# Three PSUM pairs instead of two for the first attention pass, and squares of the q/k norm moved from VectorE to ScalarE

## The chip, the cores and the metric

One Trainium2 chip, all 8 cores. Each core runs the same program on half of one batch element's queries. The metric is the device time in microseconds (us) of the slowest core. Engines: PE (TensorE), DVE (VectorE), ACT (ScalarE), POOL (GpSimd), SP (SyncE, used here for DMA).

## The reference

Two transformer layers in sequence, each attention, add, layernorm, feed-forward, add, layernorm. The change touches only the attention of layer 0:

```
q = quat_norm(quat_linear(x, qW, qb))     # r,i,j,k quarters of 256 features
k = quat_norm(quat_linear(x, kW, kb))     # each divided by sqrt(r*r + i*i + j*j + k*k + eps)
v = quat_linear(x, vW, vb)
scores = einsum(q, k) * Dh**-0.5 + const  # 16 heads of 64, 4096 keys
attn = softmax(scores);  out = einsum(attn, v)
```

The input is 4 x 4096 x 1024. A core computes 2304 query positions (2048 and a margin for the windowed attention of layer 1) against all 4096 keys.

## The kernel before, in words

The program is a list of operations for each engine, in the order in which they are appended. An engine runs its list strictly in that order; operations of different engines are joined by semaphore waits given by hand. Every VectorE and ScalarE operation also waits for the one before it on its own engine to have finished.

**The q/k stage** (`proj_norm`, called 13 times: 8 tiles of 512 positions for k, 4 of 512 and one of 256 for q). For a tile, PE makes eight output chunks `oc` of 128 features, 8 matmuls each (line 331), into PSUM banks 0 to 3 in turn. DVE takes each out with the bias into `P1FS1(oc)` (line 335), and only this frees the bank, so PE can be at most four chunks ahead. Then, for each half `h` of the 256 features of a quarter, the norm needs the sum of squares of chunks h, h+2, h+4, h+6: DVE squares chunk h into `P1FS2(h)` (line 345), then three times squares the next chunk into one temporary in PSUM bank 6 (`P1FS2(2)`, line 350) and adds it (line 353). ACT makes exp(-0.5 ln(sum + eps)) of it (lines 354 and 357). Last, DVE multiplies all eight chunks by the result of their half (line 364), in the order of `oc`, so the halves alternate. The take-outs of the next tile are behind this on DVE's list.

**Attention** (`emit_p1c(g, ...)`, called for head group g = 0 and g = 1, 8 heads each). There are 6 tiles `qt` of 384 queries, and for each 16 batches `j` (4 head pairs by 4 quarters of the keys). `emit_A(j)` is the score part: for 8 key blocks `sq`, two matmuls of 64 rows (line 506, one per head of the pair, called a score pair below) into one set of two PSUM banks, then one ACT exponential over both (line 518, 128x768) into SBUF. `emit_P(j)` is the value part: 48 matmuls of 65 columns (line 548) into bank 6 or 7. PE's order in a tile is A(0), A(1), then P(j), A(j+2) for each j, and P(14), P(15) with nothing between. The score sets alternate over two sets (banks 0, 1 and banks 2, 3): a score pair waits for the exponential that last read its set:

```python
par = (j * 8 + sq) % 2
set_base = 2 * par
if state["exp_prev"][par]:
    fw.append(state["exp_prev"][par])
```

In the pass g = 0 nothing uses banks 4 and 5. In the pass g = 1 a hook (`p2_pump`) puts the output projection, quantization and feed-forward of layer 0 between the batches, and those use banks 4 and 5. After each `qt` the result goes by DMA to DRAM (`ATT0`). Between the passes, the v projection for the second group (`emit_p1b(1, ...)`) waits for the first pass to be over. The later stages (layer 1) follow.

Of the kernel before, what the change touches and what calls it, by code (L numbers as in the profile page):

```python
# [9 lines left out]
AF = mybir.ActivationFunctionType  # L10
ALU = mybir.AluOpType
# [83 lines left out]
def build_program(stage="full"):  # L95
# [29 lines left out]
    sch = Sched()  # L125
# [3 lines left out]
    with (  # L129
# [35 lines left out]
        def P1FS1(c, n):  # L165
            return TY2.bitcast(F32)[:, 53248 // 4 + c * 512: 53248 // 4 + c * 512 + n]
# [27 lines left out]
        def PB(b, a, n, dt=None):  # L194
            if dt is not None:
# [15 lines left out]
                       waits=[tJ])  # L211
# [5 lines left out]
                      waits=[t_csum])  # L217
# [4 lines left out]
                      waits=[t_crep])  # L222
# [25 lines left out]
        def quat_bias_row(dst_off, B_ap, as_f32r_off=None, final_extra=()):  # L248
# [16 lines left out]
            if as_f32r_off is not None:  # L265
# [10 lines left out]
                       waits=[dm_chain[-1]])  # L276
# [32 lines left out]
        def proj_norm(si, n, src_fn, wbig_off, bias_col, dst_fn, extra_first=()):  # L309
            p = si % 2  # L310
            dsem = "dx0" if p == 0 else "dx1"
            tld = None
            for ic in range(8):
                wt = [stg_free[p]] if stg_free[p] else []
                tld = sch.dma("g", dsem, (lambda g, s_=src_fn(ic), d_=XSG(p, ic, 0, n):
                                          g.dma_start(out=d_, in_=s_)), waits=wt)
            ev = []
            for oc in range(8):
                bank = oc % 4
                last_mm = None  # L320
                for ic in range(8):
                    wt = []
                    if ic == 0:
                        wt = [tld] + list(extra_first)
                        if psum_free.get(bank):
                            wt.append(psum_free[bank])
                    lhsT = TEV(wbig_off, BF16, 8 * D)[:, ic * D + oc * 128: ic * D + oc * 128 + 128]
                    rhs = XSG(p, ic, 0, n)
                    last_mm = sch.op("t", (lambda t, o_=PB(bank, 0, n), l_=lhsT, r_=rhs,
                                           s0=(ic == 0), s1=(ic == 7):  # L330
                                           t.matmul(o_, l_, r_, start=s0, stop=s1)),  # L331
                                     mark=(ic == 7), waits=wt)
                ev.append(sch.op("v", (lambda v, d_=P1FS1(oc, n), p_=PB(bank, 0, n),
                                       b_=BIASB[:, bias_col + oc: bias_col + oc + 1]:
                                       v.tensor_scalar(d_, p_, b_, None, ALU.add)),
                                 waits=[last_mm]))
                psum_free[bank] = ev[-1]
            stg_free[p] = sch.op("t", lambda t: t.nop(), mark=True)

            out_toks = []  # L340
            for h in range(2):
                ssum = P1FS2(h, n)
                wt = [ev[h]] + ([norm_free[0]] if norm_free[0] else [])
                t0 = sch.op("v", (lambda v, d_=ssum, a_=P1FS1(h, n):
                                  v.scalar_tensor_tensor(d_, a_, 1.0, a_, ALU.mult, ALU.mult)),
                            waits=wt)
                for j in (2, 4, 6):
                    tmp = P1FS2(2, n)
                    sch.op("v", (lambda v, d_=tmp, a_=P1FS1(h + j, n):
                                 v.scalar_tensor_tensor(d_, a_, 1.0, a_, ALU.mult, ALU.mult)),  # L350
                           waits=[ev[h + j]])
                    t0 = sch.op("v", (lambda v, d_=ssum, a_=tmp:
                                      v.tensor_tensor(d_, d_, a_, ALU.add)))
                t2 = sch.op("s", (lambda s, d_=ssum: s.activation(d_, d_, AF.Ln,
                                                                  bias=BIASB[:, 62:63])),
                            waits=[t0, t_eps6])
                t3 = sch.op("s", (lambda s, d_=ssum: s.activation(d_, d_, AF.Exp, scale=-0.5)),
                            waits=[t2])
                out_toks.append(t3)
            final = None  # L360
            for oc in range(8):
                h = oc % 2
                final = sch.op("v", (lambda v, d_=dst_fn(oc), a_=P1FS1(oc, n), b_=P1FS2(h, n):
                                     v.tensor_tensor(d_, a_, b_, ALU.mult)),
                               waits=[out_toks[h]])
            norm_free[0] = final
            return final
# [10 lines left out]
        for sj in range(5):  # L378
            n = 512 if sj < 4 else 256
            q_done = proj_norm(  # L380
                8 + sj, n,
                (lambda ic, s_=sj, n_=n: XSF[128 * ic:128 * ic + 128, 512 * s_:512 * s_ + n_]),
                0, 0,
                (lambda oc, s_=sj, n_=n: QBUF(oc, 512 * s_, n_)))
# [12 lines left out]
        tkq_nop = sch.op("t", lambda t: t.nop(), mark=True)  # L397
# [3 lines left out]
        def quat_w2(dst_off, W_ap, firstw):  # L401
            lastv = [firstw] * 4
            tok = None
            for ic in range(8):
                comp, half = ic // 2, ic % 2
                for ob in range(4):
# [18 lines left out]
                         waits=[q_done, tkq_nop])  # L425
# [49 lines left out]
                xsg2_free = sch.op("t", lambda t: t.nop(), mark=True)  # L475
            return done, xsg2_free

        def emit_p1c(g, ready, state, hook=None):
            PVB = (6, 7)
            for qt in range(NQT):  # L480
                batches = [(hp, H, half) for hp in range(4)
# [3 lines left out]
                def emit_A(j, qt=qt, batches=batches, etoks=etoks):  # L485
                    hp, H, half = batches[j]
                    kch = g * 4 + hp
                    toks = []
                    for sq in range(8):
                        par = (j * 8 + sq) % 2  # L490
                        set_base = 2 * par
                        fw = []
                        if state["exp_prev"][par]:
                            fw.append(state["exp_prev"][par])
                        if qt == 0 and j == 0 and sq == 0:
                            fw += list(ready)
                        sub = H * 16 + half * 8 + sq
                        last = None
                        for hh in (0, 1):
                            bank = set_base + hh  # L500
                            lhsT = KBUF(kch, sub * 128, 128, p0=64 * hh, np_=64)
                            rhs = QBUF(kch, qt * QT, QT, p0=64 * hh, np_=64)
                            w = fw if hh == 0 else []
                            last = sch.op("t", (lambda t, o_=PB(bank, 0, QT), l_=lhsT,
                                                r_=rhs, tp=(64 * hh, 0):
                                                t.matmul(o_, l_, r_, start=True, stop=True,  # L506
                                                         tile_position=tp)),
                                          waits=w, mark=(hh == 1))
                        ew = [last]
                        if state["expt_free"][j % 2]:  # L510
                            ew.append(state["expt_free"][j % 2])
                        tile0 = (j % 2) * 16 + sq * 2
                        in_ap = PALL[:, set_base * 512: set_base * 512 + 1024].rearrange(
                            "p (b x) -> p b x", x=512)[:, :, 0:QT]
                        out_ap = TE[:, tile0 * QT: (tile0 + 2) * QT].rearrange(
                            "p (b x) -> p b x", x=QT)
                        etok = sch.op("s", (lambda ss, o_=out_ap, i_=in_ap:
                                            ss.activation(o_, i_, AF.Exp,  # L518
                                                          bias=BIASB[:, 63:64], scale=0.125)),
                                      waits=ew)  # L520
                        state["exp_prev"][par] = etok
                        toks.append(etok)
                    etoks[j] = toks
# [59 lines left out]
                for qs in range(3):  # L583
                    sp = sch.dma("y", "dsp", (lambda y, r0=qt * QT + qs * 128,
                                              a_=ATMv(qs * 512, 512), g_=g:
                                              y.dma_start(out=ATT0[r0:r0 + 128, g_ * 512:(g_ + 1) * 512],
                                                          in_=a_)),
                                 waits=[state["pv_norm"]])
                state["atm_free"] = sp
                if hook:  # L590
                    hook(3 * qt + 2, 4)
            return state

        st_p1c = {"exp_prev": {0: None, 1: None}, "pv_norm": None,
                  "expt_free": [None, None], "atm_free": None,
                  "pvfree": {6: None, 7: None}}
        v_done0, xf0 = emit_p1b(0, [t_vones])
        st_p1c = emit_p1c(0, [v_done0, tkq_nop, q_done], st_p1c)
        tg0 = sch.op("t", lambda t: t.nop(), mark=True)
        g0_exps = [t for t in (st_p1c["exp_prev"][0], st_p1c["exp_prev"][1]) if t]  # L600
        v_done1, xf1 = emit_p1b(1, [st_p1c["atm_free"], st_p1c["pv_norm"]])
        st_p1c["atm_free"] = xf1

# [294 lines left out]
        st_p1c = emit_p1c(1, [v_done1], st_p1c, hook=p2_pump)  # L898
# [52 lines left out]
        for ic in range(8):  # L951
# [7 lines left out]
                        waits=[l_b1q])  # L959
# [643 lines left out]
```

How the kernel before makes its waits and increments, by code:

```python
        def run(engobj, eng):  # L66
            for waits, fn, incsem, incval in self.ops[eng]:
                for (sn, sv) in waits:
                    engobj.wait_ge(sems[sn], sv)
                inst = fn(engobj)
                if incsem is not None:
                    inst.then_inc(sems[incsem], incval)
# [22 lines left out]
def build_program(stage="full"):  # L95
# [285 lines left out]
                8 + sj, n,  # L381
                (lambda ic, s_=sj, n_=n: XSF[128 * ic:128 * ic + 128, 512 * s_:512 * s_ + n_]),
                0, 0,
                (lambda oc, s_=sj, n_=n: QBUF(oc, 512 * s_, n_)))
        if stage == "p1a":
            for c in range(8):
                sch.dma("g", "dout", (lambda g, c_=c, q_=QBUF(c, 0, SPAN): g.dma_start(
                    out=DBG[:, c_ * SPAN: (c_ + 1) * SPAN],
                    in_=q_)), waits=[q_done, k_done])
            sch.op("y", lambda y: y.wait_ge(sem_handles["dout"], sch.cnt["dout"]))
            sch.emit(block, sem_handles)
            stack.close()
            return nc
# [511 lines left out]
            for sl in range(NSL):  # L906
                sch.dma("g", "dout", (lambda gg, sl_=sl: gg.dma_start(
                    out=DBG[:, sl_ * 1024: (sl_ + 1) * 1024],
                    in_=ATT0[128 * sl_:128 * sl_ + 128, :])),
                    waits=[("dsp", sch.cnt["dsp"])])
            sch.op("y", lambda y: y.wait_ge(sem_handles["dout"], sch.cnt["dout"]))
            sch.emit(block, sem_handles)
            stack.close()
```

## Time and profile before

| | us |
|---|---|
| median of 2 runs | 5560.76 (5552.95 and 5568.56) |
| the profiled execution | 5554.27 |
| its span on the slowest core (core 3) | 5552.7 |
| PE busy | 2874.3 (52%) |
| ACT busy | 1748.8 (31%) |
| DVE busy | 1641.9 (30%) |

The span runs from the first to the last instruction of a core; the profiled execution's time is 1.6 us more. No engine is near full over the whole span, because the stages have different limits, so the profile has to be read stage by stage. In what follows a window gives the busy time of each engine in a stretch, the timeline and the chain list what runs in order of time, and PEclk is the granted share of TensorE's full clock (0.50 is 1.2 GHz, 1.00 is 2.4 GHz).

### The profile page before, as it was taken

What the parts mean: (1) busy time and instruction counts of PE and PEld (TensorE: products, weight loads), DVE (VectorE), ACT (ScalarE), POOL (GpSimd) and SP (SyncE); (2) the same over time, 40 slices, a digit from 0 to 9 for tenths busy, and PEclk for the clock granted to TensorE, in tenths of its full rate; (3) what the DMA queues carried; (4) which work ended last, traced back from release to release, by engine and by line L of the source; (5) the groups of instructions that cost most, each with busy time, mean ns of one, the idle gap of its engine ahead of it and who ended that gap; (6) DMA issues with size and microseconds to landing.
All of it is one profiled execution on the core that took longest, in us unless ns stands there. A gap on an engine that the chain in (4) does not pass through costs nothing.

```text
span 5552.7 us, 63487 instructions; the slowest of 8 cores (5511.9 to 5552.7 us)
## 1 busy us (share of the span) xinstructions
PE 2874.3 (52%) x17954; PEld 1433.9 (26%) x17954; DVE 1641.9 (30%) x3602; ACT 1748.8 (31%) x2188; POOL 177.8 (3%) x339
## 2 busy tenths in 40 slices
PE   0255157777777423446464646554255554545434
PEld 0122013444444112223232323231133331212112
DVE  0477310000000113342222222224244442333444
ACT  0000007777777013335353535351023230010000
POOL 0011010000000100000000000000000000000000
PEclk9977576556556755565666665656655556666666
DMA  1322230000000320000000000000300002111000
GB/s 16 76 33 33 46 46 1 4 4 4 4 4 1 50 53 12 20 14 7 21 7 21 7 20 7 17 10 22 59 18 18 18 16 51 31 20 31 23 23 23
DMA packets 174639, 123.33 MB, mean 22 GB/s; under 512 B 106824, under 2 KB 157680, under 8 KB 174320
## 3 DMA queue, kind: packets, MB, share of 16 engines
q0 software_dynamic: 46864, 59.31, 6.4%
q1 hardware_dynamic: 127456, 59.95, 4.0%
q8 instruction: 178, 2.92, 0.2%
q14 instruction: 141, 1.16, 0.1%
HBM read 117.63 MB, written 23.59 MB: 25 GB/s over the span
## 4 chain that ended last, share of the span: by engine, by line
PE 35%; ACT 24%; DVE 17%; issue 9%; DMA 9%; SPq 3%; POOL 1%; DVEq 1%; ACTq 1%; PEldq 0%; POOLq 0%
ACT TE L518 19%; PE PALL L548 9%; PE PALL L506 4%; PE PALL L461 3%; PE PALL L331 2%; PE PALL L1143 2%; ACT TE L1119 2%; PE PALL L793 2%; PE PALL L1251 2%; DMA TY<-XFF 2%; PE PALL L1385 2%; PE PALL L1075 1%; PE PALL L1455 1%; DMA SMALL<-QBI 1%; PE PALL L714 1%
## 5 line engine op out<-in xcount | busy, mean ns | idle before, releaser
L518 ACT ACTIVATE TE<-PALL,BIASB 128x768 bf16<-128x768 f32 x1536 | 1385.6, 902 | 1068.3 <-PE PALL L506 685.2
L506 PE MATMUL PALL<-TY 64*128 64x384 bf16 x3072 | 894.6, 442 | 760.5 <-ACT TE L518 753.6
L506 PEld LDWEIGHTS PALL<-TY 64*128 64x128 bf16 x3072 | 304.0, 99 | 1298.3 <-issue 1224.7
L548 PE MATMUL PALL<-TY,TE 128*128 128x65 bf16 x9216 | 530.9, 243 | 0.0
L555 DVE RECIPROCAL SMALL<-PALL 128x6 f32<-128x6 f32 x48 | 9.4, 196 | 1738.5 <-PE PALL L548 1708.7
L548 PEld LDWEIGHTS PALL<-TY,TE 128*128 128x128 bf16 x9216 | 502.8, 131 | 59.9 <-issue 59.9
L331 PE MATMUL PALL<-TY,TE 128*128 128x512 bf16 (+1 forms) x832 | 204.5, 411 | 375.9 <-DVE TE L297 211.8
L1119 ACT ACTIVATE TE<-PALL,BIASB 128x256 bf16<-128x256 f32 (+2 forms) x240 | 155.2, 646 | 499.3 <-PE PALL L1104 480.4
L461 PE MATMUL PALL<-TE,TY 128*128 128x512 bf16 x512 | 150.7, 447 | 247.4 <-DMA TY<-XFF 247.4
L331 PEld LDWEIGHTS PALL<-TY,TE 128*128 128x128 bf16 x832 | 87.1, 107 | 493.1 <-issue 420.3
L1143 PE MATMUL PALL<-TY,TE 128*128 128x65 bf16 x864 | 130.7, 214 | 117.0 <-DVE TE L1127 115.0
L714 PE MATMUL PALL<-TE,TY 128*128 128x512 bf16 x288 | 91.7, 476 | 191.4 <-DMA TY<-ATT 173.4
L812 ACT ACTIVATE TY<-TY 128x1024 f32<-128x1024 f32 x18 | 19.0, 1057 | 481.4 <-DVE TY L808 481.4
L1127 DVE TENSOR_TENSOR TE<-TE 128x128 bf16<-128x128 bf16 (+2 forms) x480 | 133.7, 279 | 63.2 <-ACT TE L1119 13.2
L1507 ACT ACTIVATE PALL<-PALL 128x1024 f32<-128x1024 f32 x18 | 18.2, 1010 | 419.5 <-DVE PALL L1504 419.5
L1455 PE MATMUL PALL<-TY 128*128 128x512 bf16 (+1 forms) x320 | 77.1, 401 | 139.6 <-DVE TY L1439 107.5
L461 PEld LDWEIGHTS PALL<-TE,TY 128*128 128x128 bf16 x512 | 50.9, 109 | 327.7 <-issue 295.4
L471 DVE CAST TY<-PALL 128x512 bf16<-128x512 f32 x64 | 44.4, 694 | 307.5 <-PE PALL L465 290.3
L1306 PE MATMUL PALL<-IDF,TE 128*128 128x128 f32 x144 | 64.1, 445 | 136.3 <-DVE TE L1296 116.6
L1143 PEld LDWEIGHTS PALL<-TY,TE 128*128 128x128 bf16 x864 | 89.8, 104 | 159.9 <-issue 135.5
L1385 PE MATMUL PALL<-TY 128*128 128x512 bf16 (+1 forms) x320 | 85.4, 443 | 77.5 <-DVE TY L1370 77.5
L1075 PE MATMUL PALL<-TY 128*128 128x384 bf16 x384 | 77.6, 373 | 91.7 <-DMA TY<-Y2SP 91.7
(172 smaller groups left out, 2827.1 us busy)
## 6 DMA issues: line engine op xcount, KB each, us to landing
TY<-XFF POOLq DMA_DIRECT2D x192, 128.0 KB, 4.5
TY<-XST POOLq DMA_DIRECT2D x18, 512.0 KB, 4.0
YOUT<-TE SPq DMA_DIRECT2D x18, 512.0 KB, 2.6
ATT<-TY SPq DMA_DIRECT2D x36, 128.0 KB, 1.8
Y2SP<-TY SPq DMA_DIRECT2D x18, 256.0 KB, 2.0
ATT<-TY SPq DMA_DIRECT2D x18, 256.0 KB, 2.3
TE<-Y2SP POOLq DMA_DIRECT2D x18, 256.0 KB, 3.1
TY<-QW SPq DMA_DIRECT2D x32, 128.0 KB, 2.5
```

Source lines behind the costliest of these rows:

```text
L331: t.matmul(o_, l_, r_, start=s0, stop=s1)),
L461: s0=(ic == 0): t.matmul(o_, l_, r_, start=s0, stop=False)),
L506: t.matmul(o_, l_, r_, start=True, stop=True, tile_position=tp)),
L518: ss.activation(o_, i_, AF.Exp, bias=BIASB[:, 63:64], scale=0.125)),
L548: t.matmul(o_, l_, r_, start=s0, stop=False, skip_group_check=True)),
L714: s0=(ic == 0): t.matmul(o_, l_, r_, start=s0, stop=False)),
L1075: t.matmul(o_, l_, r_, start=s0, stop=s1)),
L1119: ss.activation(o_, i_, AF.Exp, bias=BIASB[:, 60:61], scale=1.0)),
L1127: v.tensor_tensor(d_, d_, m_, ALU.mult)),
L1143: t.matmul(o_, l_, r_, start=s0, stop=False, skip_group_check=True)),
L1385: t.matmul(o_, l_, r_, start=s0, stop=s1)),
L1455: t.matmul(o_, l_, r_, start=s0, stop=s1)),
```

## The change

Two independent edits.

1. In `proj_norm`, all eight squares of a tile are made by ACT (`activation` with Square) in place of DVE. The additions stay on DVE. Each addition now waits for ACT's square, and each further square, written to the same single temporary, waits for the addition before it (`t0`).
2. `emit_p1c` gets a parameter `nsets`. The pass g = 0 is called with 3, so the score pairs rotate over three sets (banks 0 to 5). The pass g = 1 keeps 2. The list of exponentials that the second group's output weights wait for gets the third set's.

```diff
-                t0 = sch.op("v", (lambda v, d_=ssum, a_=P1FS1(h, n):
-                                  v.scalar_tensor_tensor(d_, a_, 1.0, a_, ALU.mult, ALU.mult)),
-                            waits=wt)
+                t0s = sch.op("s", (lambda ss, d_=ssum, a_=P1FS1(h, n):
+                                   ss.activation(d_, a_, AF.Square)),
+                             waits=wt)
+                t0 = None
                 for j in (2, 4, 6):
                     tmp = P1FS2(2, n)
-                    sch.op("v", (lambda v, d_=tmp, a_=P1FS1(h + j, n):
-                                 v.scalar_tensor_tensor(d_, a_, 1.0, a_, ALU.mult, ALU.mult)),
-                           waits=[ev[h + j]])
+                    tsq = sch.op("s", (lambda ss, d_=tmp, a_=P1FS1(h + j, n):
+                                       ss.activation(d_, a_, AF.Square)),
+                                 waits=[ev[h + j]] + ([t0] if t0 else []))
                     t0 = sch.op("v", (lambda v, d_=ssum, a_=tmp:
-                                      v.tensor_tensor(d_, d_, a_, ALU.add)))
+                                      v.tensor_tensor(d_, d_, a_, ALU.add)),
+                                waits=[tsq] + ([t0s] if j == 2 else []))
...
-        def emit_p1c(g, ready, state, hook=None):
+        def emit_p1c(g, ready, state, hook=None, nsets=2):
...
-                        par = (j * 8 + sq) % 2
+                        par = (j * 8 + sq) % nsets
...
-        st_p1c = {"exp_prev": {0: None, 1: None}, "pv_norm": None,
+        st_p1c = {"exp_prev": {0: None, 1: None, 2: None}, "pv_norm": None,
...
-        st_p1c = emit_p1c(0, [v_done0, tkq_nop, q_done], st_p1c)
+        st_p1c = emit_p1c(0, [v_done0, tkq_nop, q_done], st_p1c, nsets=3)
```

## Rows read from the trace of the kernel before

**Rows 1.** The cores: span, mean granted clock.
```profile
core 3: 5552.7 us, clock 0.641
core 5: 5511.9 us, clock 0.650
die 0 (median of its cores): 5542.8 us, clock 0.642
die 1 (median of its cores): 5518.0 us, clock 0.650
```

**Rows 2.** Windows of core 3: q/k stage; most of the first pass.
```profile
core 3: us, PE busy (x) PEld busy (x) DVE busy (x) ACT busy (x) POOL busy (x), PEclk, DMA share, GB/s
218.00:600.00 382.00, 204.43 (x832) 86.99 (x830) 268.54 (x391) 35.67 (x53) 46.58 (x88) 0.78 0.23 29
1002.00:1815.00 813.00, 590.00 (x5108) 336.02 (x5108) 37.98 (x140) 572.86 (x636) 0.00 (x0) 0.55 0.01 4
```

**Rows 3.** Chain of one batch, first pass: start us, us, what.
```profile
1132.46 0.91 ACT TE L518
1133.37 0.14 issue
1133.50 0.60 PE PALL L506 x2
1134.10 2.76 PE PALL L548 x48
1136.86 0.64 PE PALL L506 x2
...
1137.63 0.91 ACT TE L518
```

**Rows 4.** Timeline of that batch: start us, us, engine, line [idle before <-releaser].
```profile
1127.48 7.87 ACT L518 ACTIVATE TE<-PALL,BIASB 128x768 bf16<-128x768 f32 x8 [2.29 <-PE PALL L506]
...
1128.53 0.60 PE L506 MATMUL PALL<-TY 64*128 64x384 bf16 x2 [0.57 <-ACT TE L518]
...
1133.50 0.60 PE L506 MATMUL PALL<-TY 64*128 64x384 bf16 x2 [0.39 <-ACT TE L518]
...
1134.03 2.82 PE L548 MATMUL PALL<-TY,TE 128*128 128x65 bf16 x48
...
1136.79 1.32 PE L506 MATMUL PALL<-TY 64*128 64x384 bf16 x4
...
1137.63 7.87 ACT L518 ACTIVATE TE<-PALL,BIASB 128x768 bf16<-128x768 f32 x8 [2.29 <-PE PALL L506]
```

**Rows 5.** Line 518 and its waits in the first pass, 840 to 1815.
```profile
L518 ACT ACTIVATE TE<-PALL,BIASB x764: 902/902/903, 839.8 to 1803.8; 128x768 bf16<-128x768 f32 x191
ACT TE L518 <- PE PALL L506: 210.8, 89, 4.6
```

**Rows 6.** Timeline of one q/k tile, after its last take-out but one.
```profile
322.06 0.75 DVE L335 TENSOR_SCALAR TY<-PALL,BIASB 128x512 f32<-128x512 f32 x1 [0.98 <-PEq L338]
322.36 7.07 PE L331 MATMUL PALL<-TY,TE 128*128 128x512 bf16 x32 [0.47 <-PEq L338]
...
322.92 0.69 DVE L345 SCALAR_TENSOR_TENSOR TY<-TY 128x512 f32<-128x512 f32 x1
323.71 0.70 DVE L350 SCALAR_TENSOR_TENSOR PALL<-TY 128x512 f32<-128x512 f32 x1
...
327.71 0.69 DVE L353 TENSOR_TENSOR TY<-TY,PALL 128x512 f32<-128x512 f32 x1
...
328.55 0.72 ACT L354 ACTIVATE TY<-TY,BIASB 128x512 f32<-128x512 f32 x1 [21.69 <-DVE TY L353]
...
329.36 0.63 ACT L357 ACTIVATE TY<-TY 128x512 f32<-128x512 f32 x1
...
334.94 0.63 ACT L357 ACTIVATE TY<-TY 128x512 f32<-128x512 f32 x1
335.75 1.49 DVE L364 TENSOR_TENSOR TY<-TY 128x512 bf16<-128x512 f32 x2 [0.97 <-ACT TY L357]
...
342.57 2.72 PE L331 MATMUL PALL<-TY,TE 128*128 128x512 bf16 x6 [13.15 <-DVE TY L335]
```

**Rows 7.** ACT's groups by shape over the whole span, and its table loads.
```profile
L737 ACT ACTIVATE TY<-TY 128x1024 f32<-128x1024 f32 x18 | 19.0, 1057 | 84.8 <-DVE TY L733 84.8
...
L1507 ACT ACTIVATE PALL<-PALL 128x1024 f32<-128x1024 f32 x18 | 18.2, 1010 | 419.5 <-DVE PALL L1504 419.5
...
L354 ACT ACTIVATE TY<-TY,BIASB 128x512 f32<-128x512 f32 x24 | 17.4, 724 | 297.4 <-DVE TY L353 297.4
L357 ACT ACTIVATE TY<-TY 128x512 f32<-128x512 f32 x24 | 15.1, 631 | 2.2
...
L749 ACT ACTIVATE SMALL<-SMALL,BIASB 128x1 f32<-128x1 f32 x18 | 5.3, 297 | 9.3 <-DVE SMALL L745 9.3
...
L354 ACT ACT_TABLE_LOAD x1 | 1.3, 1283 | 235.7 <-DVE TY L353 235.7
...
L357 ACT ACTIVATE TY<-TY 128x256 f32<-128x256 f32 x2 | 0.8, 418 | 0.2
```

**Rows 8.** The first pass's chain around a rise of the clock.
```profile
891.08 2.76 PE PALL L548 x48
893.84 0.64 PE PALL L506 x2
894.61 0.91 ACT TE L518
...
901.24 2.50 PE PALL L548 x48
903.74 0.48 PE PALL L506 x2
904.36 0.91 ACT TE L518
```

**Rows 9.** Windows: PE and clock before, in and after that rise.
```profile
901.20:903.36 2.16, 2.16 (x42) 2.16 (x42) 0.00 (x0) 1.19 (x2) 0.00 (x0) 0.52 0.00 0
903.36:906.70 3.34, 1.78 (x19) 0.86 (x16) 0.00 (x0) 1.88 (x3) 0.00 (x0) 1.00 0.01 2
906.80:911.20 4.40, 2.82 (x11) 0.89 (x10) 0.00 (x0) 4.03 (x5) 0.00 (x0) 0.50 0.00 0
```

More of the change, by code:

```diff
@@ L597, in build_program @@
         v_done0, xf0 = emit_p1b(0, [t_vones])
-        st_p1c = emit_p1c(0, [v_done0, tkq_nop, q_done], st_p1c)
+        st_p1c = emit_p1c(0, [v_done0, tkq_nop, q_done], st_p1c, nsets=3)
         tg0 = sch.op("t", lambda t: t.nop(), mark=True)
-        g0_exps = [t for t in (st_p1c["exp_prev"][0], st_p1c["exp_prev"][1]) if t]
+        g0_exps = [t for t in (st_p1c["exp_prev"][0], st_p1c["exp_prev"][1],
+                               st_p1c["exp_prev"][2]) if t]
         v_done1, xf1 = emit_p1b(1, [st_p1c["atm_free"], st_p1c["pv_norm"]])
```

## Prediction, made before the changed kernel was run

> **What bounds the kernel now.** I read the cores first: all within 41 us of each other, no die set apart [rows 1], so core 3 stands for all. The windows by stage came next. They show the two places that the change touches: a q/k stage of 382 us in which DVE is busy for 268.5 us and ACT for 35.7, and the first attention pass, where ACT is busy for 70% of the time and PE for 73%, neither full [rows 2]. Two engines so loaded, and taking turns, ask for the chain of one batch.
>
> The chain [rows 3] shows the turn. The exponential of key block 5 ends at 1133.37. It frees a PSUM set for the score pair of block 7 (0.60 us), behind which, on PE's list, stand the 48 value matmuls (2.76 us) and then the next batch's first score pair (0.64 us), and only then can ACT go on, at 1137.63. From the end of exponential 5 that is 4.26 us. In it ACT has just the two exponentials 6 and 7 to do. The timeline says the same: eight exponentials in 7.87 us, then 2.29 us of idle, ended by the score matmuls [rows 4]. Within the eight, ACT itself is the limit: each takes 902 ns, first to last alike [rows 5], and (7.87 - 0.90) / 7 makes a pitch of 0.995 us, while a score pair is ready for ACT 0.86 us after the exponential that freed its set has ended (0.13 to start, 0.60, 0.13 to ACT, as in the chain), and ACT is by then still at the exponential between. A batch lasts 10.15 us (1127.48 to 1137.63).
>
> In the q/k stage the chain is DVE's list. After the last take-out (ends 322.81) come 14 squares and additions of which each takes 0.69 to 0.70 us with 0.10 us between, then Ln and Exp of the second half on ACT, then the multiplications; PE meanwhile has used up its four free banks and sits idle for 13.15 us [rows 6].
>
> **The third set of banks.** With three sets the score pair of block 7 waits for exponential 4, not 5. So the value matmuls start one pitch earlier relative to ACT: from the end of exponential 4 to the next batch's first exponential it is again 4.26 us, but now there are three exponentials in it. The idle time falls from 2.29 to 1.30 us, by one pitch of 0.995 us. The price is nothing: no instruction is added, and a score pair for the third set is issued while ACT works. The same holds where a query tile ends: P(14) and P(15) stand back to back there, the idle is longer (up to 4.6 us), and it too shortens by one pitch. The trace has 89 such idle times, 210.8 us together [rows 5]; the last batch of the pass gives one more at its end. 90 x 0.995 = **-89.6 us**. The stall goes where it was, only shorter: 1.30 us per batch of ACT waiting for PE's value part, 4.26 us long against 2.99 of cover. Banks 4 and 5 are idle in this pass, and what follows it (second v projection, second pass) waits for its end and moves up with it.
>
> **The squares on ACT.** Removed from DVE are 8 squares per tile, but what was one engine's unbroken list becomes a ping-pong. The chain from the last take-out on, by the new order:
> - first half: two squares (of chunks 0 and 2) are done early, while PE still works. Then add, square, add, square, add, Ln, Exp;
> - second half: on ACT's list its first square stands behind the first half's Exp. Square, square, add, square, add, square, add, Ln, Exp; then the multiplication.
>
> That is 6 additions of 0.69, 6 squares, 2 Ln of 0.72, 2 Exp of 0.63, and the hand-overs: 6 from DVE to ACT at 0.15 (328.40 to 328.55), 6 from ACT to DVE at 0.18 (335.57 to 335.75), 4 from ACT to ACT at 0.09 (329.27 to 329.36) [rows 6]. A square of 128x512 is not in the trace. One of 128x1024 takes 1057 ns from SBUF. Exp at 512 columns takes 631 ns and at 256 columns 418, so 256 columns are worth 213 ns; the Square at 1024 less two such steps is 631, and I take 0.63. The bounds are 0.58 (1010 ns of the PSUM form less the same 426) and 0.72 (Ln's at 512) [rows 7]. The sum: 6 x 0.69 + 6 x 0.63 + 1.45 + 1.26 + 0.90 + 1.08 + 0.36 = 12.97 us. Before it was 335.75 - 322.92 = 12.83. So a tile gets 0.14 us longer; twelve tiles of 512 and one of 256, for which the same working gives 0.6, make **+2.2 us**. The 8 squares taken from DVE are hidden by nothing and gain nothing, since the chain now waits at 12 hand-overs for ACT. If a hand-over cost only 0.09 like those within an engine, it would be 12 x 13 x 0.075 = 12 us better; at 0.25, and a square at 0.72, some 13 + 7 = 20 us worse. Those are the ends.
>
> The Trainium skill ("ScalarE: Activation LUTs", Rules for kernel authors) says to use VectorE, not ScalarE, for plain arithmetic such as a product. Here the trace does not bear out a dearer element: 0.63 on ACT against 0.70 on DVE. By that rule the edit loses time, and it does so in my sum too, but through the order and not the price.
>
> **The clock.** In most batches PE runs at 1.2 GHz. In some the granted clock goes from 0.52 to 1.00 within the value matmuls, stays so for about 3.3 us, and is 0.50 again while the scores follow at ACT's pace [rows 9]. If the rise falls before the end of the value part, the part takes 2.50 rather than 2.76 us, the score pair 0.48 rather than 0.64, and the step from first exponential to first exponential is 9.75 rather than 10.15 us, 0.40 less [rows 8]. A batch of 9.16 us meets such rises at other places. I take one in ten of the 90 batches to gain it newly: **-3.6 us**; the ends are 0 and -36 (all of them).
>
> **Sum.** -89.6 + 2.2 - 3.6 = -91.0. Against the profiled execution: 5554.3 - 91.0 = 5463.3 us. The median of the two runs lies 6.5 above the profiled execution; I put half of that on top, 5466 us, 1.7% less than the median.
>
> **Rivals.**
> - *The clock stays up.* With three pairs behind the value part PE's dense stretch is some 0.6 us longer and its busy share rises from 7.58 of 10.15 to 7.6 of 9.16. If that kept 2.4 GHz through the next value part, that would take about half, 1.4 us, the 1.30 us of idle would vanish, and a batch would be 8 x 0.995 = 7.96 us: 90 x 1.2 = 108 us more, 5358 us. Against it: the five remaining score pairs are still issued at ACT's pace, 0.6 of each 1.0 us, and there the clock fell each time [rows 9]. Chance 0.07. The Trainium skill ("TensorE: Matmul & The Clock Gate", A second HAM failure mode) tells of cycling through PSUM banks that leaves TensorE idle for moments and lets its clock oscillate; the swing in these rows agrees, and by it a deeper rotation would move the kernel this way.
> - *The third set buys nothing*, because the first score pair and not the bank is what ACT waits for. The chain would have to start elsewhere than at exponential 5, and it starts there in the batches looked at [rows 3]. Then 5554.3 + 2.2 = 5556 us. Chance 0.06.
> - *Function tables.* If Square were not in the same table as Ln and Exp, ACT would reload at 1.283 us [rows 7], three times per tile on the path (the first half's change to Square is early): 13 x 3 x 1.283 = 50 us, 5516 us. Against it: Square, Ln and Exp alternate 18 times at lines 737 and 749 with no load named for them [rows 7]. Chance 0.04.
> - *Slower than before: the hand-overs.* 12 per tile, 156 in all, lie bare. They eat the whole gain when one costs 91 / 156 = 0.58 us over the 0.165 used, so from 0.75 us on, and 2% are lost from about 1.5 us on. At 0.9 it is 5578 us. No hand-over between DVE and ACT in the tile is over 0.18 [rows 6]. Chance 0.02.
>
> **Chances and range.** My forecast has 0.80, 0.01 is for what I don't see. Own range: low end from the clock's and the hand-overs' better ends in part, 5435; high end from the median's level with no gain of the clock and the squares at their worse end, 5560.8 - 89.6 + 20 = 5491, and somewhat over, 5500. That holds 8 in 10 over all cases. About 2% is what a measurement of this kernel can tell from no change, and that is 111 us: reached by the first rival and by the outer tail of my own case, 0.10 together; slower by 2%, 0.02; within, 0.88.
>
> **What would show it.** The idle before line 518 in the first pass at 1.30 us in most batches, and the score pair in front of the value part released by the exponential three before it: the step right. Idle still 2.29: wrong. The pass's total idle near 120 us. In the q/k stage 0.14 us more per tile from the last take-out to the second multiplication, squares of 0.63 us on ACT, DVE idle between additions, no new table load but one. PEclk of the first pass near 0.55 to 0.65; 0.8 or more would mean the first rival.

## The result

| | before | after |
|---|---|---|
| median | 5539.58 us (10 runs) | 5453.69 us (11 runs) |
| lowest to highest | 5530.01 to 5568.62 | 5442.27 to 5484.11 |
| ratio, 95% interval | | 0.9845 (0.982 to 0.9871) |

The changed kernel is 1.55% faster, 86 us by the medians. The forecast was 5466 us, 1.7% less than the median known then; with more runs the median of before lies 21 us lower than the two runs had shown.

The cores of after, with their spans and mean granted clocks; rows 1 are the same view of before:

```profile
core 0: 5438.1 us, clock 0.658
core 3: 5445.4 us, clock 0.660
core 7: 5450.2 us, clock 0.660
die 0 (median of its cores): 5437.5 us, clock 0.660
die 1 (median of its cores): 5441.8 us, clock 0.661
```

The spans taken by themselves mislead. Core 3 got 107 us shorter, the median core of die 1 only 76 us. Cut by stage, the two have the same gain in the same place. The first attention pass, from the first to the last start of its 768 exponentials, is the one stage that moved on every core alike, by 91.3 to 94.3 us (the short stretches between the stages are left out of the table):

| stage, us | core 3 before | core 3 after | core 7 before | core 7 after |
|---|---|---|---|---|
| q/k stage (first to last matmul) | 368.3 | 369.1 | 369.8 | 368.5 |
| first v projection, up to the first exponential | 167.0 | 172.6 | 160.1 | 173.9 |
| first attention pass | 967.9 | 876.3 | 967.4 | 875.6 |
| second pass | 1702.7 | 1701.0 | 1697.4 | 1700.6 |
| all behind it | 1793.7 | 1772.6 | 1774.3 | 1779.7 |

The rest is scatter: the v projection waits on loads of x and takes 158 to 175 us on one core or another, in the kernels below with two sets as in those with three, and what lies behind the second pass takes 1772 to 1794 us on the cores of these two kernels.

These are the windows of core 3 after, for the q/k stage and the middle of the first pass; the columns are those of [rows 2]:

```profile
218.00:600.00 382.00, 204.50 (x832) 86.71 (x830) 197.41 (x286) 97.33 (x157) 46.56 (x88) 0.78 0.22 29
900.00:1700.00 800.00, 620.63 (x5612) 366.43 (x5609) 41.79 (x154) 629.57 (x698) 0.00 (x0) 0.63 0.01 4
```

In the first line DVE has lost 71 us of busy time and ACT has gained 62 [rows 2], in a stage of unchanged length. In the second, ACT's share of the pass has gone from 70% to 79%.

The chain of one batch after (start us, us, what), to be held against [rows 3]:

```profile
1108.48 0.91 ACT TE L520
1109.40 0.14 issue
1109.53 0.60 PE PALL L508 x2
1110.13 2.75 PE PALL L550 x48
1112.89 0.64 PE PALL L508 x2
...
1113.66 0.91 ACT TE L520
```

And the timeline of ACT around it, against [rows 4]:

```profile
1104.51 7.87 ACT L520 ACTIVATE TE<-PALL,BIASB 128x768 bf16<-128x768 f32 x8 [1.29 <-PE PALL L508]
1113.66 7.87 ACT L520 ACTIVATE TE<-PALL,BIASB 128x768 bf16<-128x768 f32 x8 [1.29 <-PE PALL L508]
1122.64 2.89 ACT L520 ACTIVATE TE<-PALL,BIASB 128x768 bf16<-128x768 f32 x3 [1.11 <-PE PALL L508]
```

The chain leaves ACT at the exponential that starts at 1108.48, the fifth of the eight that begin at 1104.51, which is exponential 4. From its end to the next batch it is 4.27 us, as before; three exponentials lie under that instead of two, and the idle time is 1.29 us instead of 2.29. The third line is a batch in which the clock had risen before the value part ended: 1.11.

The timeline of one q/k tile after, from its last take-out, against [rows 6]:

```profile
324.21 0.75 DVE L335 TENSOR_SCALAR TY<-PALL,BIASB 128x512 f32<-128x512 f32 x1 [0.97 <-PEq L338]
...
325.06 0.69 DVE L354 TENSOR_TENSOR TY<-TY,PALL 128x512 f32<-128x512 f32 x1
325.90 0.60 ACT L351 ACTIVATE PALL<-TY 128x512 f32<-128x512 f32 x1 [9.30 <-DVE TY L354]
326.67 0.69 DVE L354 TENSOR_TENSOR TY<-TY,PALL 128x512 f32<-128x512 f32 x1 [0.92 <-ACT PALL L351]
...
330.65 0.63 ACT L345 ACTIVATE TY<-TY 128x512 f32<-128x512 f32 x1
331.38 0.60 ACT L351 ACTIVATE PALL<-TY 128x512 f32<-128x512 f32 x1
332.15 0.69 DVE L354 TENSOR_TENSOR TY<-TY,PALL 128x512 f32<-128x512 f32 x1 [3.18 <-ACT PALL L351]
...
337.82 5.47 DVE L366 TENSOR_TENSOR TY<-TY 128x512 bf16<-128x512 f32 x7 [0.97 <-ACT TY L359]
```

DVE now does an addition, waits 0.92 us for ACT's next square, does an addition, and so on. From the first operation behind the last take-out to the second multiplication it is 337.82 - 325.06 = 12.76 us, where it was 12.83.

### The profile page after: what moved, and what is told of

Same layout as the page of the kernel before. It is cut to its first block, busy times and chain, and to the rows that moved or that the text cites. A ratio compares the mean times of both kernels' runs of the same rounds, so it can differ in the third digit from the quotient of the medians.

```text
span 5450.2 us, 63668 instructions; the slowest of 8 cores (5427.7 to 5450.2 us)
## 1 busy us (share of the span) xinstructions
PE 2822.2 (52%) x17954; PEld 1427.4 (26%) x17954; DVE 1570.9 (29%) x3498; ACT 1807.9 (33%) x2292; POOL 177.8 (3%) x339
## 4 chain that ended last, share of the span: by engine, by line
PE 36%; ACT 24%; DVE 16%; issue 9%; DMA 9%; SPq 4%; POOL 1%; DVEq 1%; ACTq 1%; PEldq 0%; POOLq 0%
ACT TE L520 18%; PE PALL L550 10%; PE PALL L508 4%; PE PALL L463 3%; PE PALL L331 2%; PE PALL L1146 2%; DMA TY<-XFF 2%; PE PALL L796 2%; ACT TE L1122 2%; PE PALL L1254 2%; PE PALL L1078 1%; SPq L701 1%; PE PALL L1458 1%; PE PALL L1388 1%; PE PALL L717 1%
## 5 line engine op out<-in xcount | busy, mean ns | idle before, releaser
L508 PE MATMUL PALL<-TY 64*128 64x384 bf16 x3072 | 861.4, 422 | 701.2 <-ACT TE L520 689.7
L1458 PE MATMUL PALL<-TY 128*128 128x512 bf16 (+1 forms) x320 | 74.2, 390 | 139.0 <-DVE TY L1442 107.6
L1107 PE MATMUL PALL<-TY 64*128 64x128 bf16 (+2 forms) x480 | 114.0, 336 | 18.9 <-DVE TY L1082 6.8
```

The lines of the kernel that those rows point to most:

```text
L508: t.matmul(o_, l_, r_, start=True, stop=True, tile_position=tp)),
L1107: t.matmul(o_, l_, r_, start=True, stop=True, tile_position=tp)),
```

## The experiments

**Each edit alone.** `e1_sets_only` is the changed kernel with the squares put back on DVE, as they were. `e2_squares_only` is the kernel before with the squares on ACT:

```diff
 # e1_sets_only, against the changed kernel: the lines of proj_norm as before
 # e2_squares_only, against the changed kernel (the sets' other lines go back too):
-        def emit_p1c(g, ready, state, hook=None, nsets=2):
+        def emit_p1c(g, ready, state, hook=None):
...
-                        par = (j * 8 + sq) % nsets
+                        par = (j * 8 + sq) % 2
```

> The kernel before with the third set of PSUM banks alone; the squares stay on VectorE. Theory (the idle time of ScalarE per batch is the 4.26 us from the end of the last exponential that the score pair ahead of the value part waits for, less the exponentials still to do, and a third set puts one more of 0.995 us under it): the first pass goes from 968 to about 876 us, its idle times from 2.29 to 1.30 us in most batches, the whole kernel gets 92 us shorter, ratio about 0.983. Rival (part of the gain comes from the squares): the pass is shorter by the same, but the whole kernel clearly less than the changed kernel's.

> The kernel before with the squares on ScalarE alone; two sets of banks. Theory (the list of VectorE becomes a ping-pong of the same length): from the last take-out to the second multiplication of a 512 tile 12.8 us against 12.8 before, the q/k stage the same within 3 us, the whole kernel the same, ratio 1.000. Rival (hand-overs between VectorE and ScalarE cost more when they are frequent): each at 0.3 us or more, stage longer by 20 us or more, ratio 1.004 or more. Rival (VectorE, relieved of 104 operations, gets the tiles out sooner): stage shorter by more than 10 us.

Measured: the sets alone give 0.9835 (0.9809 to 0.9861), the squares alone 1.0012 (0.9997 to 1.0028); both together had given 0.9845. On core 3 the first pass is 875.9 us with the sets and 969.2 with the squares, the q/k stage 370.7 and 369.2. A tile of `e2_squares_only`, DVE only:

```profile
327.05 0.75 DVE L335 TENSOR_SCALAR TY<-PALL,BIASB 128x512 f32<-128x512 f32 x1 [0.97 <-PEq L338]
327.90 0.69 DVE L354 TENSOR_TENSOR TY<-TY,PALL 128x512 f32<-128x512 f32 x1
...
340.67 0.69 DVE L366 TENSOR_TENSOR TY<-TY 128x512 bf16<-128x512 f32 x1 [0.97 <-ACT TY L359]
```

That is 12.77 us again. So the whole gain belongs to the third set, and the squares are worth nothing that can be measured, in either direction. Both rivals about them, dear hand-overs and a relieved DVE, are out: each asked for a stage at least 10 us off. The interval of the second ratio is wide enough for a loss of 15 us, but the stage itself, 0.9 us longer on core 3 and within 2.2 us of before on every other core, does not show one.

**Is it the value part that the third set covers?** Both kernels have the squares on ACT; they differ in the number of sets. In the first pass they leave out the value matmuls of every other key block, 24 of 48:

```diff
-                    for sq in range(8):
+                    for sq in ((0, 2, 4, 6) if g == 0 else range(8)):
...
-                                                 mark=(sq == 7 and hh == 1 and qs == 2))
+                                                 mark=(sq == (6 if g == 0 else 7) and hh == 1 and qs == 2))
```

> The squares on ScalarE, two sets of banks, and in the first pass only every other key block in the value part (24 of 48 matmuls per batch; half of the values' sum is left out). Theory: the value part takes 1.38 us instead of 2.76, so ScalarE's idle time is 2.29 - 1.38 = 0.91 us in most batches, the pass about 837 us (968 less 95 x 1.38). Rival (what ScalarE waits for is the release of the banks, not the value part): idle time hardly changed, pass over 930 us.

> The same halved value part (half of the values' sum is left out) with three sets of banks. Theory: three exponentials (2.99 us) cover 4.26 - 1.38 = 2.88 us, so ScalarE has no idle time in most batches and the third set is worth only the 0.91 us that was left: pass about 766 us, 71 less than with two sets. Rival (a third set is worth one exponential of 0.995 us whatever stands before it): 90 us less than with two sets, about 747.

Measured, as ACT's waits for the score matmuls in the first pass (waited in total us, times, longest), first with two sets and the whole value part (`e2_squares_only`), then with two sets and half of it (`e3_half_value_2sets`):

```profile
ACT TE L520 <- PE PALL L508: 212.2, 89, 4.8
```

```profile
ACT TE L520 <- PE PALL L508: 92.9, 89, 2.3
```

The 89 waits are the same ones, but shorter: the median falls from 2.29 to 0.97 us, where 0.91 was expected. With three sets and half the value part hardly any are left (`e4_half_value_3sets`), and ACT's timeline has no gap over a stretch of 26 exponentials:

```profile
ACT TE L520 <- PE PALL L508: 8.2, 11, 1.3
```

```profile
1099.99 25.77 ACT L520 ACTIVATE TE<-PALL,BIASB 128x768 bf16<-128x768 f32 x26
```

On core 3 the pass is 850.0 us with two sets (837 expected) and 770.3 with three (766 expected); each kernel ran once, and its other cores lie within 1.2 us of that. The third set is worth 80 us here, not the 92 it is worth with the whole value part. The expectations had 71 for a set that gives back only what is idle and 90 for a fixed worth, so the total alone falls between them. The single waits decide. Of the 89, 84 stand inside a query tile, behind one half piece; these had 0.97 us, and the set takes away 0.88 of it, down to the 0.09 that ACT always has between two exponentials. The other 5 stand at the ends of tiles, behind two half pieces in a row, with 2.04 to 2.29 us; there the set gives its full 1.0 us and 0.93 to 1.29 stay (the longest, 1.3, is in the row above). 84 x 0.88 + 5 x 1.0 = 79 us. A set gives back one exponential, or what is idle if that is less. A fixed worth would have made it 850.0 - 92 = 758 us on this base; the 770.3 are 12 us over that.

The 13 us by which the two-set pass missed have three parts. The half piece takes 1.44 us and not 1.38 on the chain, so a wait loses 1.32. The granted clock of the pass is 0.51, so the few waits that a higher clock had shortened are shortened no more. And the pass, from its first to its last exponential, holds 94 value parts and not 95.

**What would remove the rest.** Two more kernels take the two mechanisms to their ends, on top of the changed kernel. `e5_early_squares` takes the squares off the chain (`emit_add(c)` adds the square of chunk c to the sum of its half; the waits are left out here):

```diff
+            def TMPQ(c):                      # four temporaries, banks 4 to 7
+                return PALL[:, 512 * (4 + (c - 2) % 4): 512 * (4 + (c - 2) % 4) + n]
...
                 psum_free[bank] = ev[-1]
+                if oc >= 4 and oc < 7:
+                    emit_add(oc - 2)
+                sqt[oc] = sch.op("s", (lambda ss, d_=dq, a_=P1FS1(oc, n):
+                                       ss.activation(d_, a_, AF.Square)), waits=w_)
...
-            for oc in range(8):
+            for oc in (0, 2, 4, 6, 1, 3, 5, 7):
```

`e6_interleave` writes TensorE's list of the first pass block by block, in a function of its own, `emit_p1c_il` (in short form here; G counts the batches of all query tiles):

```diff
-                emit_A(0)
-                emit_A(1)
-                for j in range(16):
-                    emit_P(j)
-                    if j + 2 < 16:
-                        emit_A(j + 2)
+            for G in range(NQT * 16):
+                for sq in range(8):
+                    pv_last = values(G, sq)       # 6 value matmuls
+                    if G + 2 < NQT * 16:
+                        scores(G + 2, sq)         # one score pair
```

`e7_all` has both, and the second order in the second pass too.

> The changed kernel, with the squares taken off the chain: ScalarE squares each chunk as soon as it is taken out, into four temporaries (banks 4 to 7) in turn, VectorE adds between the take-outs, and the multiplications of the first half stand before those of the second. Theory (the edit gained nothing because all squares but three stood behind the last take-out, in a ping-pong with one temporary): from the last take-out to the first multiplication about 3.3 us instead of about 12.8 to the second, 9.3 us less per tile, q/k stage from 369 to about 248 us, the whole kernel about 120 us shorter than the changed one, 5335 us, ratio to before 0.962. Rival (TensorE or the loads are close behind and take over): q/k stage 280 us or more.

> The changed kernel, with the first pass in another order on TensorE: the six value matmuls of one key block, then the score pair of a block two batches on, block by block, over the ends of query tiles too. Theory (ScalarE's 1.30 us of idle per batch is there because 48 value matmuls stand in one piece on TensorE's list): the idle times go, the pass is bound by 768 exponentials of 0.995 us, about 768 us instead of 875, the whole kernel about 5350 us, ratio to before 0.965. Rival (TensorE at 1.2 GHz needs 6 x 0.0575 + 0.64 = 0.99 us per block, as much as ScalarE, and any switch between the two shapes makes it the bound): pass of 820 us or more, unless its clock rises.

> Both of the above, and the block by block order in the second pass too, with its two sets of banks. Theory: the gains of the q/k stage (120 us) and of the first pass (105 us) add up, and the second pass, where ScalarE is idle 2.29 us in the batches without other work between them, gets 100 to 200 us shorter: the whole kernel at 5030 to 5130 us, ratio to before about 0.92. Rival (the second pass is bound by VectorE's quantization chain, which TensorE waits for): it stays within 40 us of 1700, the whole at about 5230 us.

| kernel | median, us | ratio to before | q/k stage, core 3 | first pass | second pass |
|---|---|---|---|---|---|
| e5_early_squares | 5351.13 | 0.9634 (0.96 to 0.9668) | 258.6 | 876.3 | 1701.4 |
| e6_interleave | 5350.66 | 0.9636 (0.9606 to 0.9667) | 371.1 | 764.5 | 1700.7 |
| e7_all | 5013.27 | 0.9021 (0.8994 to 0.9049) | 260.9 | 764.5 | 1487.8 |

In `e5_early_squares` squares and additions run between the take-outs, while TensorE works (in the changed kernel two of the eight squares stood ahead of the last take-out, not three as the expectation says):

```profile
314.02 0.69 DVE L327 TENSOR_TENSOR TY<-TY,PALL 128x512 f32<-128x512 f32 x1
314.07 0.60 ACT L361 ACTIVATE PALL<-TY 128x512 f32<-128x512 f32 x1 [1.42 <-DVE TY L346]
314.95 0.75 DVE L346 TENSOR_SCALAR TY<-PALL,BIASB 128x512 f32<-128x512 f32 x1 [0.23 <-PE PALL L342]
...
318.40 0.75 DVE L346 TENSOR_SCALAR TY<-PALL,BIASB 128x512 f32<-128x512 f32 x1 [0.18 <-PEq L362]
319.25 2.27 DVE L327 TENSOR_TENSOR TY<-TY,PALL 128x512 f32<-128x512 f32 x3
...
322.50 4.67 DVE L379 TENSOR_TENSOR TY<-TY 128x512 bf16<-128x512 f32 x6 [0.97 <-ACT TY L372]
```

Of the work behind the last take-out, two additions, an Ln and an Exp stand before the first multiplication, which starts 3.35 us after the last take-out ended (318.40 + 0.75), where 3.3 was expected. The stage falls by 110.5 us against the 121 expected (258.6 and not 248). A take-out between which DVE now also adds waits only 0.18 to 0.23 us for TensorE, so the two are nearly level there; how the missing 10 us divide over the tiles was not followed. The kernel changes three things at once, the place of the squares, the four temporaries and the order of the multiplications, and the same order with the squares left on DVE was not run. So it shows that the chain behind the last take-out sets the stage, not what each of the three is worth.

In `e6_interleave` the window of TensorE in the first pass reads:

```profile
900.00:1600.00 700.00, 698.60 (x5618) 378.83 (x5617) 41.73 (x154) 632.90 (x703) 0.00 (x0) 0.50 0.01 4
```

ACT is at 0.902 of each 0.995 us, its own pitch, and the pass takes 768 x 0.995 = 764 us. What was expected to be close is close: TensorE counts as busy for 698.6 of 700 us, at 1.2 GHz, and a block takes it as long as ACT. The rival asked for a pass of 820 us or more and is out, but nothing shows room on TensorE for more work.

`e7_all` is the best version found, 9.8% under the kernel before and 8.1% under the changed one. The gain of the second pass (213 us) is a little over the 100 to 200 expected, and the whole lies 17 us under the 5030 to 5130 expected.

**With no piece to cover, is a third set worth anything?** `e8_interleave_2sets` is `e6_interleave` with two sets:

```diff
-        st_p1c = emit_p1c_il(0, [v_done0, tkq_nop, q_done], st_p1c, nsets=3)
+        st_p1c = emit_p1c_il(0, [v_done0, tkq_nop, q_done], st_p1c, nsets=2)
```

> The block by block order in the first pass as in e6_interleave, but with two sets of banks. Theory (the third set only covers a piece of the value part, and with no such piece it has nothing to cover: a score pair is ready 0.86 us after its set is free, under the 0.995 us pitch of the exponentials): pass again about 764 us, whole kernel within 0.3% of e6_interleave. Rival (with TensorE's list nearly full the third set is needed to absorb the hand-overs): pass of 800 us or more.

The pass takes 764.7 us on core 3, against 764.5 with three sets; the one run is at 5360 us, 0.2% above the median of `e6_interleave`. ACT's timeline:

```profile
1099.30 25.75 ACT L634 ACTIVATE TE<-PALL,BIASB 128x768 bf16<-128x768 f32 x26
```

The third set, all of the measured change's gain, is worth nothing once the work stands in another order.

## Why the prediction was right

**What bounds the kernel.** Right. The chain said that the first exponential of a batch waits for everything that stands behind one freed set on TensorE's list, and the two half-value kernels show it: halve that piece, and the same 89 waits get shorter by about half of it (1.32 us of 2.76).

**The third set of banks.** Expected: idle time from 2.29 to 1.30 us, one exponential of cover more, -89.6 us; the total idle near 120 us. Found: 1.29 us, and the idle times over 0.5 us on core 3 add up to 119.7 us over 89 of them where they were 210.8 [rows 5]. The five at the ends of tiles lost one pitch too, as forecast: together 20.6 us before and 15.7 after. The pass is 91.6 us shorter on core 3, 91.3 to 94.3 on the others. The 90th idle time of the sum lies behind the last exponential and so outside the pass as measured here: 89 x 0.995 = 88.6 us belong to the pass. The price of nothing was right too: the eight exponentials still take 7.87 us.

**The squares on ACT.** Expected +2.2 us, with a chain of 12.97 us. Found 12.76. The mis-sized term is the square into PSUM: the profile has it at 602 ns (72 of them), where I had taken 631; it lay within the bounds of 0.58 and 0.72. The one whose sum stays in SBUF is at 631 exactly:

```profile
L351 ACT ACTIVATE PALL<-TY 128x512 f32<-128x512 f32 x72 | 43.4, 602 | 158.5 <-DVE TY L354 142.4 <-DVE TY L335 15.0
L345 ACT ACTIVATE TY<-TY 128x512 f32<-128x512 f32 x24 | 15.2, 631 | 291.7 <-DVE TY L335 290.6
...
L356 ACT ACT_TABLE_LOAD x1 | 1.3, 1283 | 1.0 <-DVE TY L354 1.0
```

Five of the six squares on the chain are of the shorter kind: 5 x 0.03 = 0.15 us. The hand-overs came out at 0.15 (325.75 to 325.90) and 0.17 (326.50 to 326.67) instead of 0.15 and 0.18. With both, 12.97 becomes 12.76. The stage moved by 0.8 us on core 3. The Trainium skill's rule of plain arithmetic on VectorE ("ScalarE: Activation LUTs", Rules for kernel authors), whose figure is for bf16, did not decide anything for these f32 squares: one costs 0.60 to 0.63 us on ACT and 0.70 on DVE here, and neither price set the time; the place on the chain did, as `e5_early_squares` shows.

**The clock.** Expected -3.6 us from rises of the clock met at other places, as one batch in ten at 0.40 us each. The pass shortened by 91.6 us and the third set explains 88.6, so 3.0 us are left for the clock. Its granted share of the pass went from 0.56 to 0.63 on core 3. The sum came out near, but not its factors, and one in ten was only a guess: that it fits is partly luck. Of the 84 waits inside the tiles, 30 are now shortened by a rise (under 1.25 us), where 9 were before (under 2.25). So it is one in four that gains newly, and each by 0.1 to 0.3 us, since the rise comes late: before the wait of 1.11 us shown above, the value part takes 2.73 us, nearly as ever, and only the score pair behind it is shorter, 0.48 us. The rest of a rise lies in the score part, which goes at ACT's pace.

**The rivals.** The clock staying up: 0.63, and idle times of 1.29 us, so no. Each rise of the pass ended in the score part, before the change (33 on core 3) and after (59); the prediction had shown one [rows 9]. The third set buying nothing: no, by `e1_sets_only`. Function tables: one load in the stage, at the first Ln, as before, and none at a Square in between (row above). The hand-overs: 0.15 to 0.17 us, far from the 0.75 at which they would have eaten the gain.

**The number.** 5466 us was 12 us over the median of 5453.69. The difference from before was forecast at 91 us and is 86 by the medians, with an interval of 71 to 100. Two misses make the 12 us and partly cancel. The level was 18 us too high: the sum stands on 5557.5, half way between the profiled execution and the median of the two runs then known, and ten runs gave 5539.58. The gain was 5 us too large against the medians, well inside the interval; the stage itself gave the 92 us.

## What to carry to other kernels

If a chain shows two engines taking turns, write the idle time as a sum: from the end of the last work that frees a buffer, through all that stands on the other engine's list, to the next start, less the work that is still queued. One more buffer gives back one unit of that work, and no more than is idle. Moving work between two engines that take turns gave nothing while it stayed on the same chain; moved to a place where both were waiting for a third one, it did (110 us in `e5_early_squares`). And before a buffer is added to cover a long piece, look whether the piece can be cut up: with the value matmuls block by block the third set was worth nothing, and the order alone gave more than the set.

## What the runs showed that was not expected

A TensorE that the profile counts as busy without a break stayed at half its clock. In `e6_interleave` it was busy for 698.6 of 700 us at a granted clock of 0.50, while the kernels with idle gaps and 48 value matmuls in one piece had 0.56 and 0.63. Idle gaps alone do not bring the clock up either: with 24 value matmuls in a piece, `e3_half_value_2sets` and `e4_half_value_3sets` had 0.51. The Trainium skill ("TensorE: Matmul & The Clock Gate", What's actually happening) has the clock rise after sustained activity; the trace does not agree for this mix of 64-row score matmuls and 65-column value matmuls, if busy by the profile's count is activity. That count is generous, since the profile models where a matmul ends. In each block of `e6_interleave` 0.41 us pass from the start of the second score matmul to that of the first value matmul, and 0.19 us from the last value matmul's start to the first score matmul's, against 0.05 us from one value matmul to the next. In the q/k stage, with 128x128 weights and 512 columns, the clock behaved as that section of the Trainium skill has it: 0.78 with the old chain, and 0.92 in `e5_early_squares`, where TensorE has less idle time:

```profile
220.00:475.00 255.00, 195.70 (x814) 83.31 (x813) 190.73 (x270) 94.13 (x150) 46.56 (x88) 0.92 0.32 44
```

Whether the two shapes or the changes between them keep the clock down was not tried, so it stays open.
